# One wait for a free slot of sums per four steps, and at least one step for every cell and tile

## The reference

```
edge_index = stack([src, dst])
x = layernorm(x + L0(x, src, dst, edge_weight, W, b))            # weighted sums of messages, then a dense layer
x = layernorm(x + L1(x, edge_attr_8, Wq, Wk, Wv, Wo, src, dst))  # attention with 8 heads over edges
x = layernorm(x + L2(x, relvectors, w_ih, w_hh, ..., src, dst, edge_type_16))  # GRU on sums of neighbours
x = layernorm(x + L3(x, edge_index, W1, b1, W2, b2, fc1_w, ...)) # two graph convolutions, two dense layers

L0:  msgs = edge_val[:, None] * X[edge_col];  h = segment_sum(msgs, edge_row);  h @ W.T + b
L2:  msg = h[src] + relvectors[rel];  red = segment_sum(msg, dst);  gru_cell(red, h)
```

## Time and profile before

| | us |
|---|---|
| median of three runs | 3745.39 (3744.38 to 3753.15) |
| the profiled execution, its own time | 3748.93 |
| its span, first to last instruction | 3747.1 |
| message sums, first to last matmul | 790 to 1090 |
| build, first to last step | 2525 to 2886 |
| mean granted TensorE clock over the span | 0.841 |

### The profile page before, as it was taken

The page is one execution under the profiler, slowest core; times in us unless marked ns, Lnnn a source line. Parts: engine busy times, 40 slices in busy tenths (PEclk is TensorE's granted clock), DMA queues, the critical chain, the costliest instruction groups (busy, mean ns, idle before and its releaser), DMA issues.

```text
span 3747.1 us, 53736 instructions
## 1 busy us (share of the span) xinstructions
PE 2859.3 (76%) x10760; PEld 1801.4 (48%) x10762; DVE 2199.0 (59%) x7181; ACT 680.3 (18%) x1768; POOL 1693.2 (45%) x2011
## 2 busy tenths in 40 slices
PE   1067777757778777777688887877777999998998
PEld 0043343435546444444467776643333666445654
DVE  5866666634443688888788888767776000652002
ACT  0022222200013222222100000015552000452000
POOL 0757777754420577777577777500000222002443
PEclk6588888889989888888686767657887999999999
DMA  3034422246641344443433333403332445003887
GB/s 96 32 84 112 110 101 101 101 127 202 197 126 48 88 106 107 106 107 106 72 103 103 103 104 105 78 0 121 126 127 92 140 138 146 11 1 119 273 266 232
DMA packets 317535, 423.27 MB, mean 113 GB/s; under 512 B 182658, under 2 KB 227936, under 8 KB 317062
## 3 DMA queue, kind: packets, MB, share of 16 engines
q0 software_dynamic: 105264, 324.88, 29.0%
q1 hardware_dynamic: 208072, 92.62, 9.5%
q10 hardware_dynamic: 3982, 3.24, 0.3%
HBM read 312.03 MB, written 112.79 MB: 113 GB/s over the span
## 4 chain that ended last, share of the span: by engine, by line
PE 28%; DVE 14%; issue 5%; POOL 4%; DMA 4%; ACT 3%; DVEq 1%; ACTq 0%; POOLq 0%
PE PSA L869 15%; PE PSA L993 5%; POOL G L467 4%; DVE S L1561 3%; PE PSA L1048 2%; DMA G<-tab_k,srci 2%; DMA G<-tab_v,srci 2%; DVE S L1562 2%; PE PSA L994 1%; PE PSA L1050 1%; DVE acc L1285 1%; ACT L760 1%; DVE work L1489 1%; PE PSA L947 1%; DVE stats L1290 1%
## 5 line engine op out<-in xcount | busy, mean ns | idle before, releaser
L485 POOL DMA_DIRECT2D G<-tab_A x375 | 201.5, 538 | 1095.7 <-PE PSA L869 629.9
L467 POOL DMA_INDIRECT G<-tab_k,srci x448 | 426.1, 951 | 297.1 <-DMA tab_v<-KV 160.9
L449 POOL DMA_INDIRECT tab_m<-G,posi x448 | 437.0, 975 | 176.1 <-issue 89.4
L467 POOL DMA_INDIRECT G<-tab_v,srci x448 | 435.6, 972 | 164.5 <-issue 87.1
L887 PE MATMUL PSA<-ident,oh 128*128 128x128 f32 x896 | 306.0, 342 | 225.6 <-DVE oh L1274 222.1
L993 PE MATMUL PSA<-work,oh 128*128 128x256 f32 x896 | 417.6, 560 | 39.5 <-DVE work L1489 26.7
L624 ACT COPY ohT<-PSA 128x128 f32<-128x128 f32 x896 | 237.5, 265 | 1056.2 <-PE PSA L887 1027.0
L1274 DVE TENSOR_SCALAR oh<-iota_f,dstl 128x128 f32<-128x128 f32 x1344 | 418.9, 312 | 6.5 <-DVE near L1410 0.5
L947 PE MATMUL PSA<-Q,ohT 128*128 x896 | 359.1, 492 | 17.9 <-ACT ohT L624 11.3
L896 PE MATMUL PSA<-X,ohT 128*128 x896 | 342.5, 473 | 38.4 <-ACT ohT L624 20.0
L887 PEld LDWEIGHTS PSA<-ident,oh 128*128 128x128 f32 x896 | 142.4, 159 | 459.5 <-DVE oh L1274 436.8
(11 more groups left out here) (326 smaller groups left out, 4124.2 us busy)
## 6 DMA issues: line engine op xcount, KB each, us to landing
G<-tab_A POOLq DMA_DIRECT2D x375, 320.0 KB
tab_A<-G SPq DMA_DIRECT2D x125, 320.0 KB, 2.1
G<-tab_m SPq DMA_DIRECT2D x224, 129.0 KB, 2.6
G<-tab_m POOLq DMA_DIRECT2D x224, 129.0 KB
WT<-tab_m SPq DMA_DIRECT2D x544, 1.0 KB
rec<-tab_rec SPq DMA_DIRECT2D x448, 6.5 KB
tab_m<-G,posi POOLq DMA_INDIRECT x448
G<-tab_k,srci POOLq DMA_INDIRECT x448
```

Source lines behind the costliest of these rows:

```text
L449: pool.indirect_dma_start(tab_m[0:E, :], bass.IndirectOffsetOnAxis(ap=posi[:, t:t + 1], axis=0), G[:, t % GR, :MW], None, bounds_check=E - ...
L467: pool.indirect_dma_start(G[:, t % GR, :p.w], None, p.table, bass.IndirectOffsetOnAxis(ap=srci[:, t:t + 1], axis=0)).then_inc(p.rows[t % G ...
```

## The change

The table of each stage keeps the PSUM address of all eight steps but only two counts, one for each four steps: the count that the fourth of the four steps needs. TensorE loads 10 registers per eight steps and not 16. Only steps 0 and 4 of each eight do the `& 255` and wait for a free slot; the other six wait for their one-hot alone. So a step can wait for the slot of a cell that begins up to three steps later. That the slot can come free at all needs cells and tiles that are not empty: four steps may then touch four of them at most. Hence the number of steps of a cell or tile is raised to one where it is zero. This takes the place of a plain copy and adds no instruction. For this graph no cell and no tile is empty: the smallest cell counted from the inputs has two steps, so the steps stay as they are. VectorE makes the tables with as many instructions as before, except that the count is written for 112 or 136 places and not for 448 or 544.

```diff
+        QW = U // 4
-        kz3 = kz.rearrange("p (t c) -> p t c", c=2)
+        kz3 = kz.rearrange("p (t c) -> p t c", c=QW + U)
...
-                            tz[:, 2 * t:2 * (t + U)], engines=[ET.PE], min_val=0, max_val=512 * (SLOTS + 3),
+                            tz[:, t // U * (QW + U):(t // U + 1) * (QW + U)], engines=[ET.PE], min_val=0, max_val=512 * (SLOTS + 3),
...
-                    tile, slot = at[2 * r:2 * r + 2]
-                    pe.wait_ge(p0.added, tile & 255)
+                    slot = at[QW + r]
+                    if r % 4 == 0:
+                        pe.wait_ge(p0.added, at[r // 4] & 255)
                     pe.wait_ge(p0.oh, t + 1)
...
-                        kz[:, 2 * t:2 * (t + U)], engines=[ET.PE], min_val=0, max_val=1024 * (SLOTS - 1),
+                        kz[:, t // U * (QW + U):(t // U + 1) * (QW + U)], engines=[ET.PE], min_val=0, max_val=1024 * (SLOTS - 1),
...
-                k, slot = at[2 * (t % U):2 * (t % U) + 2]
-                pe.wait_ge(b_ev, k & 255)
+                slot = at[QW + t % U]
+                if t % 4 == 0:
+                    pe.wait_ge(b_ev, at[t % U // 4] & 255)
                 pe.wait_ge(b_oh, t * 2 + 2)
...
-                link(dve.tensor_copy(small[0:NB, 1:2], smalli[0:NB, 1:2]))
+                link(dve.tensor_scalar(small[0:NB, 1:2], smalli[0:NB, 1:2], 1.0, None, ALU.max))
...
-            link(dve.tensor_scalar(tz3[:, :, 0], bs_row[1], 1, None, ALU.add))
+            bs8 = bs_row[1].rearrange("p (t u) -> p t u", u=U)
+            link(dve.tensor_scalar(tz3[:, :, 0:QW], bs8[:, :, 3::4], 1, None, ALU.add))
...
-            bl(dve.tensor_copy(bcol[0:NK, 0:1], cells))
+            bl(dve.tensor_scalar(bcol[0:NK, 0:1], cells, 1.0, None, ALU.max))
...
-            bl(dve.tensor_scalar(kz3[:, :, 0], kf, 1.0, None, ALU.add))
+            kf8 = kf.rearrange("p (t u) -> p t u", u=U)
+            bl(dve.tensor_scalar(kz3[:, :, 0:QW], kf8[:, :, 3::4], 1.0, None, ALU.add))
```

More of the change, by code:

```diff
@@ L231, in gnn_kernel @@
         b_end = rows4[:, T + 2 * T2:T + 2 * T2 + NK]
-        kz = rows4[:, T:T + 2 * T2]
-        kz3 = kz.rearrange("p (t c) -> p t c", c=2)
+        QW = U // 4
+        kz = rows4[:, T:T + T2 // U * (QW + U)]
+        kz3 = kz.rearrange("p (t c) -> p t c", c=QW + U)
         assert 2 * T2 + NK <= 3 * T
         tile_end = sb("tile_end", [1, NB], I32)
-        tz = gru[0:1, 0:2 * T].bitcast(I32)
-        tz3 = tz.rearrange("p (t c) -> p t c", c=2)
+        tz = gru[0:1, 0:T // U * (QW + U)].bitcast(I32)
+        tz3 = tz.rearrange("p (t c) -> p t c", c=QW + U)
         bcol = sb("bcol", [P, 6])
@@ L1316, in _ @@
             dve.wait_ge(pm.oh, T)
-            link(dve.tensor_scalar(tz3[:, :, 0], bs_row[1], 1, None, ALU.add))
-            link(dve.tensor_scalar(tz3[:, :, 1], bs_row[1], SLOTS - 1, None, ALU.bitwise_and))
-            link(dve.tensor_scalar(tz3[:, :, 1], tz3[:, :, 1], 9, None, ALU.logical_shift_left))
-            link(dve.tensor_scalar(tz3[:, :, 1], tz3[:, :, 1], 512 * 4, None, ALU.add))
+            bs8 = bs_row[1].rearrange("p (t u) -> p t u", u=U)
+            link(dve.tensor_scalar(tz3[:, :, 0:QW], bs8[:, :, 3::4], 1, None, ALU.add))
+            link(dve.tensor_scalar(tz3[:, :, QW:], bs8, SLOTS - 1, None, ALU.bitwise_and))
+            link(dve.tensor_scalar(tz3[:, :, QW:], tz3[:, :, QW:], 9, None, ALU.logical_shift_left))
+            link(dve.tensor_scalar(tz3[:, :, QW:], tz3[:, :, QW:], 512 * 4, None, ALU.add))
             link(dve.memset(tile_end[:, NB - 1:NB], T))
@@ L1535, in _ @@
             bl(dve.tensor_copy(kf, b_k))
-            bl(dve.tensor_scalar(kz3[:, :, 0], kf, 1.0, None, ALU.add))
-            bl(dve.tensor_copy(kz3[:, :, 1], kf))
-            bl(dve.tensor_scalar(kz3[:, :, 1], kz3[:, :, 1], SLOTS - 1, None, ALU.bitwise_and))
-            bl(dve.tensor_scalar(kz3[:, :, 1], kz3[:, :, 1], 10, None, ALU.logical_shift_left))
+            kf8 = kf.rearrange("p (t u) -> p t u", u=U)
+            bl(dve.tensor_scalar(kz3[:, :, 0:QW], kf8[:, :, 3::4], 1.0, None, ALU.add))
+            bl(dve.tensor_copy(kz3[:, :, QW:], kf8))
+            bl(dve.tensor_scalar(kz3[:, :, QW:], kz3[:, :, QW:], SLOTS - 1, None, ALU.bitwise_and))
+            bl(dve.tensor_scalar(kz3[:, :, QW:], kz3[:, :, QW:], 10, None, ALU.logical_shift_left))
             dve.sem_inc(s_("b_v"), 2)
```

## The result

The change made the kernel slower. The median is 3806.64 us (3801.06 to 3814.21) against 3746.43 us (3744.38 to 3753.15) for the kernel before: a ratio of 1.0159, interval 1.0133 to 1.0184, some 60 us. The forecast was 3675 us, and its range ended at 3702.

The account below looks back on a forecast made before the run. The prediction took TensorE's sequencer to bound the build and a ring of waits the message sums. From 3748.9 us it took 67 (build: 63 + 4) and 3 (message sums): 3679, as median 3675 us; range 3650 to 3702.

Parts of the forecast that it names:

- the register load: TensorE's sequencer, per eight steps: 10 registers take 0.72 us where 16 took 1.106, saving 0.385 us.
- The message sums: Stage bound by its ring of waits, not TensorE's sequencer: gain 3 us; rival with up to 24 us, 3655 us, 0.08.
- the ring: Message sums: VectorE waits for messages, GpSimd for TensorE's places, TensorE for one-hots; bounds the gain to 0 to 24 us.
- The clock: Build: TensorE's share rises to 0.83, level stays full, giving 4 us; rival that it stays mixed: 3694 us, 0.20 with VectorE binding.
- The ALU_OP: TensorE's sequencer, six of eight steps: each dropped one saves 0.093 us, 0.56 us per eight steps.
- The condition left out of the EVENT_SEMAPHORE: TensorE's sequencer: the EVENT_SEMAPHORE stays with one condition less, priced at nothing.
- The earlier wait: Four steps wait for their last step's slot: covered by at least eight steps; only five last cells wait, under 1 us.
- The rival of 3900 us: Build: the earlier wait binds, every cell costing the drain's 1.6 to 1.8 us: 3900 us, chance 0.03.
- the slower end: Whole kernel: chance 0.03 of being slower by more than about 0.3% (11 us), its case being the earlier wait binding.
- VectorE: Build: one-hot pairs 0.49 us apart, 3.9 us per eight, nearly full, not the bound; rival that it binds: 3694 us, 0.20 with clock mixed.
- not 295: Sign of the forecast: a build of about 295 us, with eight steps taking 4.2 to 4.4 us.

Follow-up runs that it names:

- ten registers out of rows of twelve: The changed kernel with two unread words added per table row, so every row begins at a multiple of 16 bytes: 3711.82 us, ratio 0.9905 to the kernel before.
- twelve registers: The changed kernel with four counts and eight addresses per load, rows of 48 bytes: 3689.28 us, ratio 0.9851 to the kernel before; again 3688.04 us, 0.9858.
- with 20: The changed kernel with one load of four counts and sixteen addresses per sixteen steps, both stages: 3697.35 us, ratio 0.9859 to the kernel before.
- the waits alone: The changed kernel with table rows of 16 words and 16-register loads as before; only the dropped waits and `& 255` remain: 3713.8 us, ratio 0.9917 to the kernel before.
- (eight): The kernel with twelve registers, but build counts packed into two addresses, eight registers loaded, two more ALU_OPs: 3690.97 us, again 3678.26; ratios 0.9836, 0.9825 to the kernel before.

## Why the prediction was wrong

**The step that failed** is the register load, as the prediction put it: "That is 0.064 us per register, so 10 registers take 0.72 us and 0.385 us go away per eight steps. The bounds are near: nothing in the rows lets it be under 0.36 or over 0.42." The loads took 1.08 and, in turn with that, 2.41 to 3.34 us. Per eight steps nothing went away: the mean load of the build rose from 83.5/68 = 1.23 us to 142.7/68 = 2.10. Two points, eight and sixteen registers, had been made into a line. Both are multiples of four words and both come from rows that begin at a multiple of 16 bytes. Neither says what a remainder costs or what another start costs, and the change brought both, 10 words and a row of 40 bytes. Runs gave the missing points (medians in the message sums, and of the older load):

| registers | 8 | 10 | 12 | 16 | 20 |
|---|---|---|---|---|---|
| start at a multiple of 16 bytes, us | 0.593 | 1.077 | 0.848 | 1.107 | 1.360 |
| other start, us | | 2.408 | | 3.807 | |

At a good start four more registers cost 0.255 us (0.593, 0.848, 1.107, 1.360), and the two left over of ten cost (1.077 - 0.593)/2 = 0.24 each. At another start each register costs (3.807 - 2.408)/6 = 0.233. So the load seems to go by four words where it can and else word by word. The prediction held the Trainium skill's about 200 ns per register (Runtime: NRT & Kernel Launch, Instruction fetch mechanics) against 1.107 us for 16 and set it aside. Loads at other starts come near that figure (3.807 us for 16, 0.238 each), loads at a good start don't (0.069 each); the page ties its price to no start, and whether its own loads had such starts no run here shows. Where a page and a row differ by a factor of three, both may be right under different conditions, and the question is which condition the new code meets.

**The sum, with this one term put right.** The build: 408 ALU_OPs at 0.093 us take away 38 us, and the loads add 59.2, which is 21 more; 27 to 29 were measured, and the 6 to 8 between them were not traced. The message sums: 35.9 us more of loads; 29.6 were measured. Whether the ring took in the rest can't be told, since the stage scatters by as much from one execution to the next. Waits in the message sums of the kernel after, beside the earlier trace rows:

```profile
POOL G L462 <- PE PSA L858: 192.4, 174, 3.7
DVE oh L1331 <- DMA G<-tab_m: 123.0, 135, 3.4
...
PE PSA L858 <- DVE oh L1331: 101.4, 74, 28.0
```

TensorE waits for one-hots 74 times and not 30, but their number explains no loss: with ten registers out of rows of twelve it waits 82 times and the stage takes 299.4 us, as before. It is the time that differs, 101.4 us and 76.4 there. So with the long loads TensorE loses the load itself and then waits longer for one-hots as well; the order of cause in this ring is argued and not shown. The forecast had bounded only what the ring does with a gain (0 to 24 us). What it does with a loss was not asked.

**The clock.** The level was to rise to full because TensorE's busy share would rise to 0.83, above the 0.78 of the message sums. In the kernel after the share fell (256.58 of 392 us, 0.65) and the level stayed (0.80). With fewer and shorter gaps the level did rise, but not for that reason: with twelve registers the share is 225.60 of 300, 0.75, at a level of 0.96, and with 20 it is 238.34 of 304, 0.78, at only 0.88. Share and level don't go together in these windows, so the rise that the forecast expected of its design came, but the reason it gave isn't borne out; as far as that goes it was luck. Between eight and twelve registers the level tells nothing: single executions of such builds gave 0.96 to 0.98 and 0.96 to 0.99.

**What held.** *The ALU_OP:* 0.093 us was the estimate. With the waits alone the shortest eight steps go from 5.129 to 4.556 us, 0.573 for six of them, 0.095 each; and in the build's records 0.093 us pass from the start of an ALU_OP to the start of the EVENT_SEMAPHORE behind it. *The condition left out of the EVENT_SEMAPHORE* saves nothing: from its start to that of the next instruction it is 0.151 us with two conditions and with one. *The earlier wait* cost next to nothing: in the changed kernel and in the one with twelve registers one gap of 0.65 us each could be traced to it, among the short cells. The rival of 3900 us fell, and the slower end, which had 0.03, came by a mechanism that none of the rivals named. *The message sums* gain little, as the forecast had it: no more than these runs can tell. *VectorE* isn't the bound: with twelve registers the shortest eights take 4.310 us, less than with sixteen by 0.246, so nearly all of the 0.259 that the load saves comes through. Its own pace had been read too slow, though. The 0.49 us of the earlier trace rows is TensorE's pace, which it follows there; where it runs ahead it starts a pair every 0.46 us (2699.66 to 2700.12 above), so eight take 3.7 us and not 3.9, and there was more room than was thought. The forecast's own design thus exists in near forms: with rows that begin well it takes 3689 and 3688 us (twelve registers), and 3691 and 3678 (eight), all inside the range, though with builds of 307 and 300 us and not 295. The design on the chip was another.

**What stays open.** Loads last longer in the build than in the message sums (2.92 against 2.41 us for the long ones, 1.18 against 1.08 for the short). In the last stretch of the build of the kernel after they are short again; first its single line, then its window:

```profile
L1042 PEldq TENSOR_LOAD <-rows x4: 1074/1748/2413, 2923.3 to 2938.8; - x4
```

```profile
2922.00:2945.00 23.00, 16.06 (x71) 8.07 (x69) 16.67 (x68) 0.00 (x0) 0.00 (x0) 0.80 0.00 1
```

VectorE works on there (16.67 of 23 us), but ScalarE drains no cell and nothing is written to `tab_A`. Loads of the kernel before tell these two apart. First a load under which ScalarE is busy and no packet moves, its line and its window; then one under which ScalarE is idle and a cell is being written:

```profile
L1040 PEldq TENSOR_LOAD <-rows x1: 1102/1102/1102, 2649.4 to 2649.4; - x1
...
2649.36:2650.46 1.10, 0.67 (x3) 0.08 (x1) 1.10 (x6) 1.07 (x2) 0.00 (x0) 0.67 0.00 0
...
L1040 PEldq TENSOR_LOAD <-rows x1: 1497/1497/1497, 2540.2 to 2540.2; - x1
...
2540.24:2541.74 1.50, 0.59 (x3) 0.08 (x1) 1.18 (x5) 0.00 (x0) 0.00 (x0) 0.79 0.56 215
```

So it is over all of that build: after the first, 12 loads have no packet of such a write under them, six of these with ScalarE busy for more than half of the load, and all take 1.102 to 1.107 us; every one of the 29 that take longer than 1.107 has packets under it (26 more have some and don't take longer). The longer loads go with the write of a cell and not with ScalarE's drain. It isn't transfers as such, since loads in the message sums keep their 1.106 us at a DMA share of 0.69; no run took the write away, so that it is the cause isn't shown, nor how it would be. How a load reads its words was only argued from its times. And why the message sums lose as much with half of the loads long as with all of them wasn't settled.

## What to carry to other kernels

Price a register load by where it begins and by its whole groups of four words, not by its registers: pad each row to a multiple of 16 bytes, or pack values until the row fits. A price drawn through two points holds for what those points have in common; before using it, list what the new shape does not share with them (remainder, stride, start). And read a median that lies far from the minimum and the maximum as a sign of two kinds, and print the instructions one by one.

## What the runs showed of the hardware

Not expected was that ten registers take longer than twelve (1.077 and 0.848 us), and that the start of a row alone makes a load of 16 registers 3.4 times as long (1.107 to 3.807 us), enough for 8% of this kernel. Nor that one gap of TensorE per sixteen steps, with a load of 1.36 us or more in it, goes with a granted clock of 0.88, and two gaps with loads of 0.85 with 0.96, at nearly the same work in the same time (1087 matmul records in 304 us, and 1060 in 300). Nor that a load of registers lasts longer while a cell is being written from SBUF to HBM: 1.497 us with such packets under it and 1.102 without, for 16 registers.
